# Two gated attention and feed-forward layers: split low-rank passes, one ring of three accumulator banks, and a new order of every engine's steps

## The chip, the cores and the metric

The kernel runs on one core of a Trainium2 chip. The metric is the device time of one execution in microseconds (us). A measurement of this kernel can tell a change from no change at about 0.2%.

## The reference, cut to what matters

The input `x` is 2 batches of 2048 tokens with 512 features; a context of 128 tokens per batch is given beside it. Four steps follow one another, each added to the stream with a gate:

```python
x = x + tanh(g_xattn[0]) * attention(layernorm(x), ctx)        # 8 heads, rotary, 128 keys
x = x + tanh(g_ffn[0])   * ffn_0(layernorm(x))                 # below
x = x + tanh(g_xattn[1]) * (layernorm(x) @ W1.T + mean(ctx) @ W2.T + b)
x = x + tanh(g_ffn[1])   * ffn_1(layernorm(x))                 # quantised, gelu
# ffn_0: h = ternary(w_fc)(x) + gate * (x @ v.T @ fast_b.T @ u.T);  r = relu(h);  ternary(w_proj)(r * r)
# ffn_1: h = gelu(bitlinear(x, w1, b1));  bitlinear(h, w2, b2)   # both inputs rounded to integers per token
```

The hidden width of both feed-forward parts is 2048, and the rank of the low-rank term in `ffn_0` is 16.

## The kernel before, in words

**Groups and stages.** The 4096 tokens are cut into 16 groups of 256, each of two tiles of 128 tokens. Every group goes through the same steps. On PE they are: `q` (two, queries), `s` (scores of all heads), `pv` (two, probabilities times values), `wo` (two, output projection), `low` (the low-rank rows), `up` (eight pairs of 128 hidden rows), `down` (eight pieces, four for each tile), `wx` (two, the linear step), `w1` (eight units of 512 hidden columns, four for each tile) and `w2` (two). Precision is kept by carrying most values as two f16 parts. `wx`, `w1` and `w2` are called the back stage; it trails the attention by about two groups, so that three groups are in work at a time.

**The order is written by hand.** The table `ORDER` (from line 328) gives each step of each group a place in the sequence of its engine: a row for each kind of step, in it one tuple for each group, and in the tuple a place for each step. `PREP` does so for the one-time work on the weights, which is mixed into the first groups. Each engine's `run()` walks its places in ascending order. An engine does its steps strictly in this order; a step that waits holds up all behind it. Cross-engine waits are in the helpers: `need(engine, semaphore, per, g, k)` waits until item k of group g is done, `need_dma` the same for transfers. All transfers, among them the transposes that bring a result back as a matmul input (`xT1`, `p`, `xT2`, `xT3`, `q4T`, `hT`), are issued by SP in its own order.

**Accumulator banks.** PSUM has eight banks of 512 f32 columns. Banks 0 and 1 belong to `up` and `down` (FFN0), and bank 1 takes `low` first. The attention uses 2, 3, 4 and 7 (`ATT`, `ROW_TILES`): the four score banks are 4, 7, 2, 3, and bank 7 holds nothing but the second score bank. The back stage uses 5 and 6 in turn: `wx` tile 0 and 1, `w1` units 0 to 7, `w2` tile 0 and 1. So `w1` unit u waits until DVE has emptied unit u-2 (`h_done`, L1491), and `wx` of group g waits until DVE has emptied `w2` of group g-1 (`out_done`, L1527). In the last group, where the attention is over, the back stage uses the four attention banks.

**The path through `up`.** `low` (L1744) fills bank 1; ACT copies it (L971), DVE subtracts and splits it into bf16 parts (L1420 to L1425), and `low_done` is set. Each half of an up pair is eight matmuls over `xT2` (L1764) and one low-rank matmul (L1768), so the first half of pair 0 ends with a wait for `low_done`. ACT empties a pair by two Relu (L981), and then makes two squares of it (L986, L992); pair m may start when the Relus of pair m-2 are done. POOL makes the low part of the square (L763), which `down` waits for. A score bank is emptied by a maximum on DVE (L1381), a small scale (L1385) and four Exp on ACT (L949, `s_exp`).

**Ends of a group.** `wo` is added to the input by DVE (L1407, `x1_done`), normalised, split, and transposed by DMA into `xT2`, which `low` and `up` need. `wx` is added by DVE (L1449), normalised, rounded and transposed into `q4T`, which `w1` needs (L1814). `w1`'s results go through Gelu (L1003), a maximum (L1075), rounding (L1502), a conversion (L1035) and a transpose into `hT`, which `w2` needs (L1830).

## Time and profile before

| what | value |
|---|---|
| median of 3 runs | 1218.28 us (1217.88 to 1218.72) |
| profiled execution | 1217.09 us |
| its span, first to last instruction | 1215.3 us |
| granted TensorE clock, mean | 0.977 |
| busy: PE, DVE, ACT, POOL | 91%, 79%, 65%, 49% |

The profiled execution is 1.19 us under the median, and its span is 1.8 us shorter than its own time. PE means the matmuls, PEld the weight loads that run beside them, DVE is VectorE, ACT is ScalarE, POOL is GpSimd, SP issues the transfers. An arrow in a row names what ended the idle time before an instruction. Matmul rows overlap by the drain of the array: 16 matmuls of 512 columns show 3.62 us, and the next row starts 3.45 us after their start.

### The profile page before, as it was taken

What the parts mean: (1) busy time and instruction counts of PE and PEld (TensorE: products, weight loads), DVE (VectorE), ACT (ScalarE), POOL (GpSimd) and SP (SyncE); (2) the same over time, 40 slices, a digit from 0 to 9 for tenths busy, and PEclk for the clock granted to TensorE, in tenths of its full rate; (3) what the DMA queues carried; (4) which work ended last, traced back from release to release, by engine and by line L of the source; (5) the groups of instructions that cost most, each with busy time, mean ns of one, the idle gap of its engine ahead of it and who ended that gap; (6) DMA issues with size and microseconds to landing.
All of it is one profiled execution on the core that took longest, in us unless ns stands there. A gap on an engine that the chain in (4) does not pass through costs nothing.

```text
span 1215.3 us, 22111 instructions
## 1 busy us (share of the span) xinstructions
PE 1099.9 (91%) x8254; PEld 681.4 (56%) x8542; DVE 959.9 (79%) x1993; ACT 795.2 (65%) x1557; POOL 590.3 (49%) x569
## 2 busy tenths in 40 slices
PE   5766888999999998999999989999999999999995
PEld 5544646565656555564657565654756566564642
DVE  4696689887889797888978897888869677877766
ACT  3887847666675848485756749484675929494624
POOL 2442556454546455464645465554546364563440
PEclk9878999999999999999999999999999999999997
DMA  9959472433427362435434452624345261433132
GB/s 322 361 157 280 148 195 47 95 82 81 105 48 140 57 133 55 104 80 100 88 66 105 66 128 51 126 60 102 71 79 122 48 139 34 102 70 78 23 61 65
DMA packets 281225, 129.93 MB, mean 107 GB/s; under 512 B 254992, under 2 KB 255504, under 8 KB 279440
## 3 DMA queue, kind: packets, MB, share of 16 engines
q1 hardware_dynamic: 280560, 127.57, 45.6%
q8 instruction: 66, 1.08, 0.4%
q10 hardware_dynamic: 560, 0.96, 0.3%
q14 instruction: 39, 0.32, 0.1%
HBM read 57.19 MB, written 8.39 MB: 54 GB/s over the span
## 4 chain that ended last, share of the span: by engine, by line
PE 42%; ACT 23%; DVE 22%; DMA 6%; issue 4%; POOL 3%; SPq 0%; ACTq 0%; DVEq 0%
PE ps L1780 12%; ACT e L949 5%; PE ps L1731 5%; PE ps L1814 4%; PE ps L1682 4%; PE ps L1830 4%; ACT rl L981 4%; PE ps L1764 4%; ACT hid L986 3%; ACT sq L992 2%; DVE st L1342 2%; DVE amax L1075 2%; PE ps L1797 2%; ACT p L957 1%; DMA pt<-p 1%
## 5 line engine op out<-in xcount | busy, mean ns | idle before, releaser
L1764 PE MATMUL ps<-xT,fcT 128*128 128x256 f16 x2048 | 258.7, 274 | 10.0 <-ACT rl L981 9.9
L738 POOL TENSOR_TENSOR rs<-ve,nhalf 128x1 f32<-128x1 f32 x160 | 103.8, 651 | 327.5 <-DVE ve L1347 231.0
L1780 PE MATMUL ps<-pjT,hid 128*128 128x512 fp8e4 x1024 | 232.7, 379 | 5.0 <-issue 2.7
L1764 PEld LDWEIGHTS ps<-xT,fcT 128*128 128x128 fp8e4 x2048 | 199.4, 98 | 49.0 <-ACT rl L981 13.7
L763 POOL TENSOR_TENSOR hid<-sq,hid 128x512 f16<-128x512 f32 x128 | 156.5, 1226 | 104.0 <-ACT sq L992 103.3
L1780 PEld LDWEIGHTS ps<-pjT,hid 128*128 128x128 f16 x1024 | 97.7, 98 | 98.1
L1814 PE MATMUL ps<-w1T,q4T 128*128 128x512 fp8e4 x480 | 118.5, 380 | 9.1 <-DVE h L1491 5.0
L981 ACT ACTIVATE rl<-ps,rsf 128x256 f32<-128x256 f32 x256 | 106.4, 468 | 29.7 <-PE ps L1768 29.5
L949 ACT ACTIVATE e<-ps,nmb,sig 128x128 f32<-128x128 f32 x256 | 113.1, 459 | 16.8 <-DVE nmb L1385 16.7
L1830 PE MATMUL ps<-w2T,hT 128*128 128x512 fp8e4 x480 | 108.4, 379 | 7.3 <-DMA hT<-q 7.3
L1491 DVE SCALAR_TENSOR_TENSOR h<-ps,dqs,b1bc 128x512 f32<-128x512 f32 x120 | 87.9, 743 | 25.8 <-PE ps L1814 24.8
L768 POOL TENSOR_TENSOR e<-e,einv 128x512 f32<-128x512 f32 x64 | 72.0, 1129 | 60.6 <-DVE einv L1389 60.5
L1035 ACT ACTIVATE q<-h 128x2048 f16<-128x2048 f32 x30 | 57.2, 1908 | 66.3 <-DVE h L1502 66.3
L1682 PE MATMUL ps<-pt,wq 128*128 128x256 f16 x768 | 88.6, 276 | 6.1 <-issue 4.1
L1797 PE MATMUL ps<-wx,xT 128*128 128x512 f16 x360 | 82.7, 379 | 10.0 <-DMA xT<-x16b 5.4
L1731 PE MATMUL ps<-wo,qT 128*128 128x512 f16 x384 | 85.8, 379 | 2.8 <-DVE qT L1355 2.8
L1682 PEld LDWEIGHTS ps<-pt,wq 128*128 128x128 f16 x768 | 75.4, 99 | 20.3 <-issue 10.0
L1075 DVE TENSOR_REDUCE amax<-h 128x1 f32<-128x2048 f32 x30 | 68.4, 2281 | 23.2 <-ACT h L1003 23.2
L1355 DVE TENSOR_TENSOR p<-e,p 128x512 f16<-128x512 f32 x64 | 64.2, 1014 | 25.1 <-ACT p L957 24.9
L986 ACT ACTIVATE hid<-rl 128x512 f16<-128x512 f32 x128 | 80.6, 630 | 5.0
L992 ACT ACTIVATE sq<-rl 128x512 f32<-128x512 f32 x128 | 78.5, 613 | 0.0
L1830 PEld LDWEIGHTS ps<-w2T,hT 128*128 128x128 f16 x480 | 46.1, 98 | 50.9
(234 smaller groups left out, 2032.8 us busy)
## 6 DMA issues: line engine op xcount, KB each, us to landing
xb<-in_x SPq DMA_DIRECT2D x16, 512.0 KB, 4.0
xa<-in_x SPq DMA_DIRECT2D x15, 512.0 KB, 4.0
out<-r SPq DMA_DIRECT2D x30, 256.0 KB, 2.1
rope<-in_rope SPq DMA_DIRECT2D x16, 384.0 KB, 3.4
h<-in_w1T SPq DMA_DIRECT2D x6, 1024.0 KB, 5.5
h<-in_w2T SPq DMA_DIRECT2D x6, 1024.0 KB, 5.6
h<-in_wkvT SPq DMA_DIRECT2D x2, 1024.0 KB, 12.8
hid<-in_w_fc SPq DMA_DIRECT2D x2, 1024.0 KB, 10.9
```

Source lines behind the costliest of these rows:

```text
L738: pool.tensor_tensor(rs[:, n, t:t + 1], ve[:, n, t:t + 1], nhalf[:, :], ALU.pow).then_inc(done, 1)
L763: pool.tensor_tensor(flat[:, 1, :], sq[:, m % 2, :], flat[:, 0, :], ALU.subtract).then_inc(hid_lo, 1)
L949: last = act.activation(e[:, n, a * S:(a + 1) * S], s_bank(n)[:, a * S:(a + 1) * S], ACT.Exp, bias=nmb[:, n, a:a + 1], scale=sig[:, :], ac ...
L981: act.activation(rl[:, m % 2, a * G:(a + 1) * G], ps[:, FFN0 + m % 2, a * G:(a + 1) * G], ACT.Relu, scale=rsf[:, 2 * m + a:2 * m + a + 1]) ...
L986: act.activation(hid[:, 0, 2 * m:2 * m + 2, :].rearrange("p c n -> p (c n)"), rl[:, m % 2, :], ACT.Square)\
L1682: mm = pe.matmul(q_bank(hg)[:, a * G:(a + 1) * G], wq[:, ws, k, c:c + P], xT1[:, xs, k, :], start=(n == 0 and k == 0), stop=(n == 2 and k ...
L1731: mm = pe.matmul(wo_bank(t), ao[:, xs, k, t * P:(t + 1) * P], wo[:, ws, k, :], start=(n == 0 and k == 0), stop=(n == 2 and k == KC - 1))
L1764: pe.matmul(dst, fcT[:, k, f * P:(f + 1) * P], xT2[:, xs, k, :], start=(xs == 0 and k == 0), stop=False)
L1780: mm = pe.matmul(ps[:, FFN0 + t, :], hid[:, xs, c, t * P:(t + 1) * P], pjT[:, c, :], start=(c == 0 and xs == 0), stop=(c == FC - 1 and xs ...
L1797: mm = pe.matmul(mix_bank(g, t), xT3_of(g)[:, xs, k, t * P:(t + 1) * P], wx[:, ws, k, :], start=(n == 0 and k == 0), stop=(n == 2 and k == ...
L1814: mm = pe.matmul(mix_bank(g, 2 + u), q4T_of(g)[:, k, t * P:(t + 1) * P], w1T[:, k, n * 512:(n + 1) * 512], start=(k == 0), stop=(k == KC - 1))
L1830: mm = pe.matmul(mix_bank(g, 10 + t), hT_of(g)[:, t, c, :], w2T[:, c, :], start=(c == 0), stop=(c == FC - 1))
```

## The change

Three things are done, and every order is written anew.

1. **Parted pairs.** `up` of pairs 0 and 1 does only the eight `xT2` passes of its first half. A new step `up_rest` with a place of its own waits for `low_done` and does the low-rank pass of the first half and the whole second half. Pair 0 no longer needs `low` before it in the order (it waits for `xT2` itself). Pair 1 still waits until the low-rank rows have left bank 1 (`low_r`). Pairs 2 to 7 are as before.
2. **One ring of three banks.** Banks 5, 6 and 7 form a ring in which each group has 13 slots: slot 0 is the second score bank of the group two ahead, slots 1 and 2 are `wx`, 3 to 10 are `w1`, 11 and 12 are `w2`. `w1` unit u now waits for unit u-3; unit 0 waits until ACT has done the Exp of the second score bank of the group two ahead (`s_exp` of group g+2, item 1), units 1 and 2 for `wx` of their tiles. `scores` gets a wait for the last `w1` unit of three groups before. Groups 0 and 1 keep bank 7 for their scores. In the last group the back stage has three banks (2, 3, 4) where it had four.
3. **Orders.** All places in `ORDER` and `PREP` are set anew, on all engines, with SP's transfers. PE has 630 places where it had 598. The instructions are the same in kind and number, and so are the transfers.

The diff, with the order tables cut to the rows spoken of:

```diff
@@ -168,7 +168,9 @@
         def q_bank(hg):
             return ps[:, ATT[hg], :]
 
-        def s_bank(j):
+        def s_bank(g, j):
+            if j == 1 and g >= 2:
+                return back_bank(g - 2, 0)
             return ps[:, ROW_TILES[j], :]
 
         def pv_bank(a):
@@ -177,8 +179,9 @@
         def wo_bank(t):
             return ps[:, (3, 4)[t], :]
 
-        def back_bank(n):
-            return ps[:, BACK0 + n % 2, :]
+        def back_bank(g, slot):
+
+            return ps[:, BACK0 + (13 * g + slot) % 3, :]
 
 
         hid32 = hid[:, :, :, :].rearrange("p s c n -> p (s c n)").bitcast(F32)
@@ -220,7 +223,7 @@
             return hT
 
         def mix_bank(g, n):
-            return ps[:, ATT[n % 4], :] if final(g) else back_bank(n)
+            return ps[:, 2 + n % 3, :] if final(g) else back_bank(g, 1 + n)
 
         h32 = h[:, :, :].rearrange("p t n -> p (t n)")
         hT32 = hT[:, :, :, :].rearrange("p t c n -> p (t c n)").bitcast(F32)
@@ -327,225 +330,228 @@
 
         ORDER = dict(
             PE=dict(
...
-                s=((13,), (35,), (58,), (94,), (132,), (167,), (201,), (237,), (273,), (312,), (344,), (384,),
-                   (420,), (452,), (493,), (524,)),
...
-                low=((31,), (57,), (90,), (124,), (162,), (198,), (234,), (270,), (305,), (343,), (376,), (415,),
-                     (450,), (486,), (523,), (557,)),
-                wx=((53, 56), (91, 98), (125, 135), (163, 172), (199, 204), (235, 242), (271, 276), (307, 317),
-                    (342, 352), (381, 386), (412, 422), (451, 456), (485, 495), (522, 530), (558, 560), (585, 586)),
...
-                w2=((86, 96), (123, 130), (159, 170), (195, 203), (231, 239), (267, 274), (302, 315), (339, 348),
-                    (375, 385), (408, 413), (447, 453), (483, 484), (518, 528), (555, 556), (584, 587), (596, 597))),
+                up_rest=((35, 36), (63, 64), (97, 99), (133, 134), (173, 175), (209, 212), (250, 252), (288, 291),
+                         (326, 327), (363, 364), (402, 403), (438, 441), (478, 480), (515, 516), (554, 555),
+                         (591, 593)),
+                up=((33, 34, 37, 38, 39, 40, 41, 42), (60, 62, 65, 66, 67, 68, 71, 72),
+                    (93, 98, 100, 101, 104, 105, 109, 110), (131, 132, 135, 137, 143, 144, 145, 146),
...
+                s=((13,), (31,), (61,), (102,), (141,), (179,), (215,), (249,), (287,), (328,), (366,), (405,),
+                   (444,), (481,), (525,), (556,)),
...
+                wo=((25, 27), (53, 54), (85, 86), (123, 124), (163, 165), (199, 200), (236, 237), (275, 277),
+                    (312, 313), (352, 353), (390, 391), (427, 428), (467, 468), (504, 505), (544, 545), (579, 583)),
+                low=((32,), (59,), (94,), (130,), (169,), (206,), (247,), (284,), (320,), (359,), (397,), (435,),
+                     (475,), (512,), (550,), (588,)),
+                wx=((57, 58), (96, 108), (136, 142), (168, 183), (214, 219), (246, 256), (285, 293), (324, 333),
+                    (365, 371), (396, 409), (440, 447), (472, 483), (510, 517), (552, 560), (587, 589), (617, 619)),
+                w1=((69, 70, 75, 76, 78, 79, 80, 81), (106, 107, 111, 112, 116, 119, 121, 122),
+                    (151, 152, 153, 155, 160, 161, 162, 164), (182, 186, 187, 188, 195, 196, 198, 201),
+                    (220, 221, 222, 225, 229, 230, 240, 241), (262, 263, 264, 265, 267, 268, 273, 276),
+                    (294, 297, 300, 301, 305, 310, 314, 318), (334, 335, 341, 342, 343, 344, 347, 349),
+                    (374, 375, 376, 379, 382, 383, 384, 385), (414, 415, 416, 417, 418, 419, 420, 432),
+                    (448, 450, 451, 453, 457, 458, 459, 461), (486, 487, 489, 490, 491, 492, 494, 496),
+                    (529, 531, 532, 533, 535, 536, 539, 546), (561, 564, 565, 567, 568, 570, 571, 576),
+                    (596, 597, 598, 599, 604, 605, 606, 607), (620, 621, 622, 623, 624, 625, 626, 627)),
+                w2=((90, 103), (129, 140), (167, 181), (205, 216), (243, 254), (281, 289), (319, 331), (355, 369),
+                    (394, 406), (433, 445), (469, 477), (506, 511), (549, 558), (585, 586), (616, 618), (628, 629))),
...
@@ -946,7 +952,7 @@
                     act.wait_ge(c_kap, 1)
                 need(act, s_bias, 4, g, n)
                 for a in range(4):
-                    last = act.activation(e[:, n, a * S:(a + 1) * S], s_bank(n)[:, a * S:(a + 1) * S], ACT.Exp,
+                    last = act.activation(e[:, n, a * S:(a + 1) * S], s_bank(g, n)[:, a * S:(a + 1) * S], ACT.Exp,
                                           bias=nmb[:, n, a:a + 1], scale=sig[:, :], accum_out=esum[:, n, a:a + 1])
                 last.then_inc(s_exp, 1)
 
@@ -1377,7 +1383,7 @@
 
             def soft_max(g, n):
                 need(dve, s_ps, 4, g, n)
-                scores = s_bank(n).rearrange("p (h s) -> p h s", h=4)
+                scores = s_bank(g, n).rearrange("p (h s) -> p h s", h=4)
                 dve.tensor_reduce(nmx[:, n, :], scores, axis=AX.X, op=ALU.max, negate=True).then_inc(s_max, 1)
                 if first(g) and n == 0:
                     dve.wait_ge(c_kap, 1)
@@ -1691,6 +1697,10 @@
                     pe.wait_ge(c_klo, 1)
                 if g == 1:
                     pe.wait_ge(c_mean, 1)
+                if g == 2:
+                    pe.wait_ge(c_quantp, 32)
+                else:
+                    need(pe, h_done, 4 * TILES, g - 3, 4 * TILES - 1)
                 need(pe, x1_done, TILES, g - 1, 1)
                 need(pe, q_lo, 2, g, 1)
                 b = g // PER_BATCH
@@ -1700,7 +1710,7 @@
                         for m, (half, qs, ks) in enumerate(HALVES_AND_PARTS):
                             for j in range(4):
                                 rows = slice(32 * j, 32 * j + 32)
-                                mm = pe.matmul(s_bank(j)[:, at:at + S], qT[rows, qs, hg, half, t * P:(t + 1) * P],
+                                mm = pe.matmul(s_bank(g, j)[:, at:at + S], qT[rows, qs, hg, half, t * P:(t + 1) * P],
                                                k_rows[rows, ks, 2 * hg + half, b * S:(b + 1) * S],
                                                start=(m == 0), stop=(m == 5), tile_position=(32 * j, 0))
                                 if hg == 1 and t == 1 and m == 5:
@@ -1756,17 +1766,34 @@
                     need(pe, low_r, 2, g, 0)
                 else:
                     need(pe, relu, FC, g, 2 * m - 3)
-                for a in range(2):
-                    f = 2 * m + a
-                    dst = ps[:, FFN0 + m % 2, a * G:(a + 1) * G]
-                    for xs in range(2):
-                        for k in range(KC):
-                            pe.matmul(dst, fcT[:, k, f * P:(f + 1) * P], xT2[:, xs, k, :], start=(xs == 0 and k == 0),
-                                      stop=False)
-                    if m == 0 and a == 0:
-                        need(pe, low_done, 1, g, 0)
-                    mm = pe.matmul(dst, lowA[:, f * P:(f + 1) * P], tlow[:, :], start=False, stop=True)
-                mm.then_inc(up_ps, 1)
+                if m == 0:
+                    for t in range(TILES):
+                        need_dma(pe, xT2_in[t], g)
+                up_passes(g, m, 0)
+                if m >= 2:
+                    up_rest(g, m)
+
+            def up_passes(g, m, a):
+
+                f = 2 * m + a
+                for xs in range(2):
+                    for k in range(KC):
+                        pe.matmul(ps[:, FFN0 + m % 2, a * G:(a + 1) * G], fcT[:, k, f * P:(f + 1) * P], xT2[:, xs, k, :],
+                                  start=(xs == 0 and k == 0), stop=False)
+
+            def low_pass(g, m, a):
+
+                f = 2 * m + a
+                return pe.matmul(ps[:, FFN0 + m % 2, a * G:(a + 1) * G], lowA[:, f * P:(f + 1) * P], tlow[:, :],
+                                 start=False, stop=True)
+
+            def up_rest(g, m):
+
+                if m < 2:
+                    need(pe, low_done, 1, g, 0)
+                low_pass(g, m, 0)
+                up_passes(g, m, 1)
+                low_pass(g, m, 1).then_inc(up_ps, 1)
 
             def down(g, t, piece_of_4):
                 if first(g) and piece_of_4 == 0:
@@ -1787,8 +1814,10 @@
                 if first(g) and t == 0:
                     pe.wait_ge(c_wlo, 3)
                     pe.wait_ge(c_mx, 5)
+                if first(g) and t == 1:
+                    need(pe, s_exp, 4, 1, 1)
                 if final(g):
-                    need(pe, x1_done, TILES, g, t)
+                    need(pe, x1_done, TILES, g, 1)
                 else:
                     need(pe, out_done, TILES, g - 1, t)
                 need_dma(pe, xT3_in[t], g)
@@ -1802,11 +1831,13 @@
                 u = 4 * t + n
                 if first(g) and u == 0:
                     pe.wait_ge(c_clip, 4)
-                ring = 4 if final(g) else 2
+                ring = 3
                 if u >= ring:
                     need(pe, h_done, 4 * TILES, g, u - ring)
                 elif u >= ring - 2:
                     need(pe, x3_done, TILES, g, u - ring + 2)
+                elif not final(g) and not final(g + 1):
+                    need(pe, s_exp, 4, g + 2, 1)
                 if n == 0:
                     need_dma(pe, q4T_in[t], g)
                 pe.ldweights(q4T_of(g)[:, 0, t * P:(t + 1) * P], tile_position=(0, 0))
@@ -1818,7 +1849,7 @@
             def w2_down(g, t):
                 if first(g) and t == 0:
                     pe.wait_ge(c_clip, 8)
-                need(pe, h_done, 4 * TILES, g, t + (4 if final(g) else 6))
+                need(pe, h_done, 4 * TILES, g, t + 5)
                 if final(g):
                     need_dma(pe, hT_half_in[2 * t], GROUPS)
                 else:
@@ -1834,6 +1865,8 @@
                 for p in moments("PE"):
                     for m, g in due("PE", "up", p):
                         up(g, m)
+                    for m, g in due("PE", "up_rest", p):
+                        up_rest(g, m)
                     for n, g in due("PE", "down", p):
                         down(g, n // 4, n % 4)
                     for hg, g in due("PE", "q", p):
```

## Rows read from the trace of the kernel before

**Rows 1.** The page's busy times: us, share of the span, instructions.
```profile
PE 1099.9 (91%) x8254; PEld 681.4 (56%) x8542; DVE 959.9 (79%) x1993; ACT 795.2 (65%) x1557; POOL 590.3 (49%) x569
```
**Rows 2.** Windows: length, busy of PE, PEld, DVE, ACT, POOL, PE clock, DMA share, GB/s.
```profile
0.00:100.00 100.00, 67.30 (x420) 49.89 (x420) 65.73 (x145) 70.52 (x140) 33.23 (x39) 0.86 0.85 279
100.00:200.00 100.00, 79.55 (x701) 53.19 (x710) 76.31 (x136) 69.02 (x127) 48.60 (x40) 0.93 0.60 170
200.00:1150.00 950.00, 905.22 (x6924) 556.49 (x7179) 777.66 (x1621) 628.43 (x1245) 492.52 (x475) 1.00 0.42 85
1150.00:1216.00 66.00, 47.80 (x214) 21.84 (x234) 40.19 (x93) 27.22 (x49) 15.91 (x17) 0.88 0.28 60
```
**Rows 3.** PE's waits: waiting line, what it waited for, us in total, times, longest.
```profile
PE ps L1764 <- ACT rl L981: 9.9, 10, 2.0
...
PE ps L1830 <- DMA hT<-q: 7.3, 7, 2.2
...
PE ps L1814 <- DVE h L1491: 5.0, 8, 1.4
PE ps L1797 <- DVE r L1527: 4.4, 3, 2.4
...
PE ps L1768 <- DVE tlow L1425: 3.3, 5, 0.9
...
PE ps L1780 <- ACT rl L981: 2.3, 4, 0.9
```
**Rows 4.** The tile rl: ACT's work for an up pair, ns min/median/max.
```profile
L981 ACT ACTIVATE rl<-ps,rsf x256: 452/465/518, 127.1 to 1154.8; 128x256 f32<-128x256 f32 x128
L986 ACT ACTIVATE hid<-rl x128: 629/630/632, 128.0 to 1155.3; 128x512 f16<-128x512 f32 x128
L992 ACT ACTIVATE sq<-rl x128: 612/613/617, 128.5 to 1155.8; 128x512 f32<-128x512 f32 x128
```
**Rows 5.** Timeline of PE, two up pairs in a row in the last group.
```profile
1131.53 1.04 PE L1764 MATMUL ps<-xT,fcT 128*128 128x256 f16 x8
...
1133.49 1.04 PE L1764 MATMUL ps<-xT,fcT 128*128 128x256 f16 x8
```
**Rows 6.** Timeline of PE: a `wx` that waits for its bank, a low-rank pass for `low_done`.
```profile
801.95 1.25 PE L1797 MATMUL ps<-wx,xT 128*128 128x512 f16 x5 [2.38 <-DVE r L1527]
...
931.89 0.28 PE L1768 MATMUL ps<-tlow,lowA 128*128 128x256 bf16 x1 [0.94 <-DVE tlow L1425]
```
**Rows 7.** Timeline, group 2 and group 9: the scores, and the last Exp of the second score bank.
```profile
185.65 1.52 PE L1703 MATMUL ps<-k,qT 32*128 32x128 f16 x96 [0.36 <-DVE qT L1355]
...
203.21 0.46 ACT L949 ACTIVATE e<-ps,nmb,sig 128x128 f32<-128x128 f32 x1
...
659.41 1.52 PE L1703 MATMUL ps<-k,qT 32*128 32x128 f16 x96
...
667.77 0.47 ACT L949 ACTIVATE e<-ps,nmb,sig 128x128 f32<-128x128 f32 x1
```
**Rows 8.** Timeline of the head: DVE's maximum of the `wo` weights, PE's first `wo` and `low`.
```profile
45.60 2.25 DVE L1075 TENSOR_REDUCE wmax<-pjT 128x1 f32<-128x2048 f32 x1
...
100.89 5.34 PE L1731 MATMUL ps<-wo,qT 128*128 128x512 f16 x24 [1.74 <-DVE qT L1355]
...
120.50 2.72 PE L1744 MATMUL ps<-xT,vrep 128*128 128x256 f16 x12 [5.12 <-DMA xT<-x16f]
```
**Rows 9.** Timeline of PE: the last back stage, from its first `wx` to the end.
```profile
1172.72 2.75 PE L1797 MATMUL ps<-wx,pt 128*128 128x512 f16 x12 [0.79 <-DMA pt<-x16a]
1177.51 2.75 PE L1797 MATMUL ps<-wx,pt 128*128 128x512 f16 x12 [2.04 <-DMA pt<-x16a]
1180.10 3.62 PE L1830 MATMUL ps<-w2T,hT 128*128 128x512 fp8e4 x16
1183.55 3.62 PE L1814 MATMUL ps<-w1T,qT 128*128 128x512 fp8e4 x16
1187.82 3.63 PE L1814 MATMUL ps<-w1T,qT 128*128 128x512 fp8e4 x16 [0.65 <-DMA qT<-x16a]
```

More of the change, by code:

```diff
@@ L453, in build @@
                        (514, 515)),
[L454 to L457 removed]
+                low=((56,), (86,), (114,), (145,), (176,), (207,), (242,), (271,), (301,), (331,), (362,), (393,),
+                     (425,), (457,), (488,), (517,)),
@@ new lines, in build @@
+                x2_lo=((24, 30), (52, 53), (80, 81), (113, 115), (147, 150), (182, 183), (217, 219), (252, 253),
+                       (285, 286), (319, 321), (353, 354), (387, 388), (421, 423), (454, 455), (490, 491),
+                       (520, 523)),
+                x3_lo=((47, 50), (83, 88), (111, 118), (145, 155), (180, 189), (214, 223), (247, 257), (282, 291),
+                       (316, 328), (350, 364), (384, 393), (418, 430), (451, 460), (485, 497), (519, 524),
+                       (542, 545)),
@@ new lines, in build @@
+                rot=((10, 11), (27, 29), (54, 55), (86, 87), (128, 129), (156, 159), (190, 192), (224, 225),
+                     (258, 259), (292, 293), (324, 325), (360, 361), (394, 395), (428, 429), (469, 470),
+                     (493, 494)),
+                norm=((14, 15, 16, 17), (32, 34, 41, 42), (59, 65, 69, 71), (96, 97, 99, 103), (132, 134, 139, 140),
[3 rows of a table added]
+                rs2=((22, 23), (48, 51), (76, 77), (112, 114), (146, 148), (178, 181), (212, 215), (248, 249),
+                     (280, 283), (314, 317), (348, 351), (382, 385), (416, 419), (452, 453), (488, 489),
+                     (517, 521)),
@@ L532, in build @@
                        (335, 336))))
         PREP = dict(
-            PE=dict(k=(2, 3), v=(5, 6), low=(0,), mix=(15,), tern=(4, 10, 12, 14, 17, 19, 20, 21), low_t=(18,),
-                    row_scale=(24,), mean=(30,), spread=(1, 9, 11, 16, 23)),
-            DVE=dict(ctx_sum=(11,), rot_k=(9, 10), wq_max=(4,), wq_scale=(5,), k_max=(12,), wq_lo=(7,), v_max=(17,),
-                     kv_scale=(20,), k_lo=(29,), v_lo=(34, 35), low_copy=(6,), thr=(8, 14, 21, 31, 39, 48, 49, 50),
-                     wo_max=(22,), v_top=(23,), wo_scale=(25,), wo_lo=(28,), mix_row=(43,), low_rank=(32,),
-                     v_parts=(26,), wx_max=(44,), hidden=(53,), wx_scale=(55,), wx_lo=(59,), row_scale=(57,),
-                     mean=(67,), diag=(54,), round=(68, 73, 76, 80, 86, 102, 103, 109),
-                     clip=(71, 78, 79, 94, 95, 111, 115, 116)),
@@ L542, in build @@
-            ACT=dict(wq=(3,), k_hi=(17,), v_hi=(20, 22), tanh=(0,), wo=(15,), evac=(6, 13, 16, 23, 28, 36, 37, 38),
-                     rows=(4, 7, 11, 19), whole=(5, 8, 14, 21), low=(32,), wx=(42,),
-                     sums=(27, 33, 40, 43, 44, 45, 46, 47), lift=(52, 55, 58, 74, 75, 79, 81, 85)),
-            POOL=dict(whole=(14, 19, 20, 21), rot_k=(4, 5), csb=(6,), low_zero=(13,)),
-            SP=dict(u=(1,), rows=(6,), ctx=(0,), wk=(3,), wq=(2,), wv=(7,),
-                    piece=(4, 8, 14, 20, 19, 16, 22, 24, 25, 27, 31, 34, 35, 26, 30, 38, 39, 40, 45, 46, 48, 53, 54, 58),
-                    wo=(15,), wc=(11,), wx=(5,), b1=(18,)))
+            PE=dict(k=(1, 3), v=(4, 7), low=(0,), mix=(14,), tern=(5, 8, 12, 16, 19, 20, 21, 24), low_t=(17,),
+                    row_scale=(22,), mean=(30,), spread=(2, 9, 11, 15, 26)),
@@ new lines, in build @@
+            DVE=dict(ctx_sum=(5,), rot_k=(8, 11), wq_max=(3,), wq_scale=(9,), k_max=(15,), wq_lo=(12,), v_max=(18,),
+                     kv_scale=(20,), k_lo=(29,), v_lo=(31, 32), low_copy=(6,), thr=(10, 17, 22, 38, 47, 49, 50, 51),
+                     wo_max=(7,), v_top=(21,), wo_scale=(23,), wo_lo=(26,), mix_row=(40,), low_rank=(39,),
+                     v_parts=(24,), wx_max=(43,), hidden=(54,), wx_scale=(59,), wx_lo=(67,), row_scale=(56,),
+                     mean=(70,), diag=(55,), round=(73, 76, 81, 85, 88, 90, 111, 121),
+                     clip=(75, 84, 87, 89, 96, 97, 119, 123)),
@@ new lines, in build @@
+            ACT=dict(wq=(4,), k_hi=(15,), v_hi=(18, 19), tanh=(1,), wo=(14,), evac=(6, 10, 17, 27, 35, 36, 37, 40),
+                     rows=(3, 7, 11, 20), whole=(5, 9, 13, 26), low=(30,), wx=(43,),
+                     sums=(32, 38, 41, 42, 45, 46, 49, 51), lift=(54, 57, 60, 64, 75, 76, 85, 90)),
+            POOL=dict(whole=(18, 19, 20, 21), rot_k=(5, 6), csb=(4,), low_zero=(12,)),
+            SP=dict(u=(2,), rows=(7,), ctx=(0,), wk=(3,), wq=(1,), wv=(6,),
+                    piece=(5, 10, 15, 19, 18, 17, 21, 23, 26, 30, 32, 33, 36, 29, 37, 38, 41, 42, 46, 47, 48, 50, 54, 55),
+                    wo=(4,), wc=(13,), wx=(12,), b1=(16,)))
```

217 lines of the change are left out of this document (99 added, 118 removed), and 118 rows, old and new, of tables (down, exp, h, hid).

## The prediction, made before the changed kernel was seen to run

> **What bounds the kernel now.** I read the page's busy times first, then busy times by stretch, then what PE waited for, then the timeline around those waits. PE is busy 91% of the span, DVE 79% [rows 1]. The stretches differ [rows 2]. From 200 to 1150 us PE is busy 905.2 of 950 us at a granted clock of 1.00: what is idle there is 44.8 us, and no more than that can be won by better order. The first 200 us hold 53.1 us of idle and clocks of 0.86 and 0.93; the last 66 us hold 18.2 us. So PE sets the time, and the change takes no matmul away. It can only remove waits of PE. Those waits are many and small [rows 3]: Relu on ACT (9.9 us in 10 waits, and 2.3 in front of `down`), the transposed Gelu output (7.3), a `w1` bank that DVE has not emptied (5.0), a `wx` bank still held by `w2` (4.4), `low_done` (3.3). The longest are about 2 us.
>
> How I compare two orders: PE's table says which steps lie between a step and the one that needs its result, and the spacing of rows says how long they take. Two halves of an up pair start 1.96 us apart [rows 5], 16 matmuls of 512 columns take 3.45 us, 12 take 2.59 [rows 9]. I call this the **cover** of a result. Where it is shorter than the way over the other engines, PE waits. The ways' lengths are those of this trace; under another order they may be other, which is the main doubt.
>
> **The change, part by part.**
>
> *Parted pairs.* In the first half of pair 0 PE waits for `low_done` in five groups, 3.3 us in all, 0.94 in the longest [rows 3, 6]. Now the first half of pair 1 can lie there too, 8 of an up pair's 18 matmuls, 0.87 us [rows 5]. But the new order uses this in part to pack the steps tighter: in groups 0, 3, 5 and 13 `low`, both first halves and the rest follow each other with nothing else between, so 1.7 us cover `low_done` where before mostly 2.3 to 3.5 us did. Bounds: gain 3.3, loss 2 (four groups short by 0.5). I take a gain of 1.
>
> *Relu waits.* ACT needs 2 x 0.465 + 0.630 + 0.613 = 2.17 us for a pair [rows 4], PE makes one in 1.96 [rows 5]: pairs in a row, or Exp between them on ACT, put ACT behind. For each group I set PE's cover of each pair against ACT's work in its order up to the Relu that is needed. Before, ACT comes out behind in groups 2, 4, 7, 8, 9, 11, 12 and 15 by 0.8 to 3.4 us each, 13 us with the small ones; after, from group 2 on, only by 0.7 at most, 3 us in all. Groups 0 and 1 get worse, from 9 to 12.5 us. Together 22 us short become 15. The trace paid 12.2 for the 22 [rows 3], so a third less is worth 4. Bounds: 0 and 7.
>
> *Third bank.* `w1` unit u now needs unit u-3. Where two units follow each other, cover was one unit, 0.86 us, against DVE's emptying; now it is two, 1.73 us. Of 5.0 us I take 3 (bounds 0 and 5.0). The `wx` wait of 4.4 us is three places where `w2` tile 1 stands directly before `wx` tile 1, as at 801.95 [rows 3, 6]. The ring does not remove that need, the new order does: one place with nothing between is left (`w2` tile 0 of group 2 before `wx` of group 3). Gain 3, bounds 0 and 4.4.
>
> The rows show waits of many kinds, and the two on banks are 9.4 us of them [rows 3]. The Trainium skill (Perfetto Trace Analysis, Optimization Strategy) says that one gap repeating on the engine that should be saturated can mean too few buffers in SBUF or PSUM. By that rule the third bank alone could be worth up to the steady stretch's whole idle time; by the rows it is worth at most a fifth of it, and the trace does not agree that one gap repeats.
>
> *Gelu output.* The cover of `w2` tile 1 from the last `w1` unit averages some 4 us more in the new order. Of 7.3 us [rows 3] I take 3, bounds 0 and 7.3.
>
> *The new wait.* `w1` unit 0 of group g now waits for the second score bank's Exp of group g+2. The way from the end of the scores (start plus 1.52) to the end of that Exp was 7.3 us in group 9 and 16.5 in group 2 [rows 7]; ten of the sixteen are over 8. The new order's covers are 5.4 us twice (groups 3 and 12: one up pair and one `w2` tile in group 3), 7.4, 8.0, 8.5 and ten or more in the others. In these five groups ACT's new order puts the two Exp next to each other, as in group 9, so I take 7.3: 1.9 + 1.9, with the rest near nothing 3.5. Behind the waiting unit stand `wx`, `up` and `down`, all of which wait with it. Bounds: 2 and 15 (at 9.9 us, about the middle of the sixteen). The wait added to the scores is for a `w1` unit at least 15 us back and costs nothing; cover gone, it would cost one DVE pass.
>
> *Closer inputs.* `low` of group 4 stands 7.8 us of work behind `wo` (one `down` piece, `w2`, `wx`), and in groups 5 and 14 9.5. Bounds: nothing, and the 14.3 us that lie between the end of `wo` and `low` in the head [rows 8], 6.5 us for group 4. I take a loss of 2.5, which also stands for `q` of group 2 directly behind `wo`.
>
> *Head.* DVE's maximum of `wo` (2.25 us, rows 8) leaves the stretch between the first queries and scores, its low-rank preparation goes behind the first softmax maxima, and POOL's rounding behind the normalising. The weights' load is issued earlier on SP in exchange for another of its size. The first `wo` (100.89) could start up to 7 us earlier. The rounding of `w1` and `w2` and the loads it waits for stay as long, and the head's later waits hang on them; I take 3, bounds -2 and 7. The scores of group 1 now stand ahead of the first `low`, 1.45 us, in idle that was there [rows 8].
>
> *Tail.* `w2` of group 14 now lies between the last two `wx`. The first ends at 1175.3, the second starts 3.45 us later at 1178.8 instead of 1177.51, ends at 1181.4, and unit 4 of `w1` comes 7.7 us after that, as from 1180.10 to 1187.82 [rows 9]: 1189.1, a loss of 1.3. The fourth bank, now missing there, costs nothing: two units cover a DVE pass.
>
> *SP's and POOL's queues* are renumbered by a few places, no transfer is added; nothing in both ways, and the range carries it.
>
> **Sum.** Gains 1 + 4 + 3 + 3 + 3 + 3 = 17, losses 3.5 + 2.5 + 1.3 = 7.3, net 9.7. The profiled execution took 1217.09, its span 1215.3. It becomes 1207.4; the median lies 1.2 higher: **1208.6 us**.
>
> **Rivals.** (1) *The waits only move.* PE is dense, and a wait removed lets it run into the next one, which no count by pairs of steps sees. For it: 44.8 us are spread over dozens of small waits. Against it: the gaps I name have cover to spare afterwards. Gains and losses cancel: 1217 to 1219. (2) *Slower, by the new wait.* If ACT reaches the second Exp 11 us after the scores, the places with less cover lose 3.6, 5.6, 1.0, 3.0, 2.5, 5.6 and 1.1 us, 22.4 in all, 18.9 more than taken: 1227.5. It decides from a way of about 9.5 us on; under 8 it does not. For it: the way was longer than that in most groups [rows 7]. Against it: the Exp pairs stand close in ACT's new order. (3) *Much faster*: Relu, ring, Gelu and head terms at their upper bounds, 1190 to 1197; here belongs the rule above.
>
> **How the numbers follow.** The forecast's case, 1197 to 1216, gets 0.62, rival 3 0.08, rival 1 0.13, rival 2 and kindred losses 0.17. About 0.2%, 2.4 us, is what a measurement of this kernel can tell. The range 1197 to 1222 leaves out rival 3 and about 0.1 above. Faster 0.70, same 0.13, slower 0.17.
>
> **What would show it.** PE's waits by kind: Relu under 9 us, DVE's `h` under 2.5, `wx` on DVE's output under 2, `low_done` 2 to 3, and a new line, the `w1` line waiting for ACT's Exp, at 3 to 4 us in two to five places. The first `wo` at 94 to 99 us. The window 200 to 1150 with over 910 us of PE busy at clock 1.00. The last `w1` unit 1 us later against the last `wx`. The prediction is wrong if the Exp line is over 12 us, or if the sum of PE's idle from 200 us on has not fallen.

## The result, and the profile after

The median fell from 1218.08 us (four runs beside it) to **1190.7 us** (1189.36 to 1192.99): a ratio of 0.9777, 95% interval 0.976 to 0.9794. I had forecast 1208.6 and a range from 1197. The direction was right, but the time lies outside that range: the gain was 27.4 us where I had summed 9.7.

The profiled execution took 1189.36 us, its span is 1187.5 where it was 1215.3. Busy times of the page, then windows as in [rows 2]:

```profile
PE 1095.1 (92%) x8254; PEld 681.5 (57%) x8542; DVE 951.4 (80%) x1993; ACT 794.7 (67%) x1557; POOL 592.7 (50%) x569
```
```profile
0.00:100.00 100.00, 70.68 (x442) 50.45 (x443) 67.85 (x148) 72.08 (x141) 33.16 (x40) 0.90 0.83 278
100.00:200.00 100.00, 79.55 (x714) 55.03 (x722) 79.61 (x146) 72.48 (x140) 54.29 (x45) 0.91 0.61 174
200.00:1150.00 950.00, 924.78 (x7024) 568.00 (x7291) 780.03 (x1641) 635.93 (x1245) 501.24 (x482) 1.00 0.42 87
```

From 200 to 1150 us PE is busy 924.8 us instead of 905.2, at the same clock. The instructions are the same in number, and PE needs 4.8 us less busy time for them [rows 1]. So the 27.8 us of the span are 23.0 of idle and 4.8 of busy time. Part of the latter is the clock: between 60 and 130 us 48 query matmuls take 5.40 us, the time that they take at full clock, where they took 7.07, and the granted clock of the first 100 us is 0.90 where it was 0.86. From 100 to 200 us it is 0.91 where it was 0.93, and 1.00 in the long stretch of both. That the clock is the whole of the 4.8 is not shown.

PE's waits of the kernel after, as in [rows 3]:

```profile
PE ps L1781 <- ACT rl L987: 11.3, 10, 2.2
...
PE ps L1728 <- DMA pt<-p: 8.2, 4, 6.3
...
PE ps L1861 <- DMA hT<-q: 4.7, 5, 1.4
PE ps L1713 <- DVE qT L1361: 4.6, 4, 2.9
...
PE ps L1845 <- DVE hid L1497: 3.1, 2, 1.5
...
PE ps L1845 <- DVE h L1497: 1.6, 3, 0.7
...
PE ps L1826 <- DVE r L1533: 1.2, 1, 1.2
PE ps L1754 <- DMA xT<-x16f: 1.1, 1, 1.1
...
PE ps L1845 <- ACT e L955: 0.9, 1, 0.9
...
PE ps L1787 <- DVE tlow L1431: 0.7, 2, 0.5
...
PE ps L1845 <- DMA q4T<-x16b: 0.3, 1, 0.3
PE ps L1807 <- ACT rl L987: 0.3, 1, 0.3
```

Every kind that I had named fell, Relu least. The new line, `w1` on ACT's Exp, holds 0.9 us in one wait. The row `DVE hid L1497` is also a wait for a `w1` bank: in the last group DVE writes its result into `hid`, and with three banks there `w1` waits 3.1 us that it did not wait before.

Of the signs that I had named, the first `wo` (95.11), the long stretch (924.8 us busy), `wx` on DVE's output (1.2) and the later last `w1` unit (14.6 us after the last `wx` where it was 12.9) came. DVE's `h` is at 1.6, but at 4.7 with the last group. Relu at 11.6 (forecast under 9), `low_done` at 0.7 (2 to 3) and the Exp line at 0.9 in one place (3 to 4 in two to five) did not come as said. The same view of the kernel before has kinds that I had seen and not priced:

```profile
PE ps L1703 <- DVE qT L1355: 7.8, 7, 4.1
...
PE ps L1797 <- DMA xT<-x16b: 5.4, 3, 2.7
PE ps L1744 <- DMA xT<-x16f: 5.1, 1, 5.1
...
PE ps L1797 <- DMA pt<-x16a: 2.8, 2, 2.0
...
PE ps L1814 <- DMA q4T<-x16b: 2.8, 5, 1.0
```

The two waits of `wx` (L1797) for transposes have no row after, and the other three fell from 15.7 to 6.0. Against that the head now waits 6.3 us for the first transposed probabilities (L1728); before, no such wait was longer than 0.4.

Where along the run the lead arises is read from the starts of the same steps in two timelines. `wo` of group 0 starts at 95.11 instead of 100.89 [rows 8]; `low` of group 0 is 0.7 us earlier, of group 2 8.3, of group 4 9.9, of group 8 17.4, of group 12 23.4, and `down` of the last group 27.8. So the first groups bring 8 to 10 us, groups 4 to 15 bring 18, and the last back stage brings nothing. In a second execution of the same kernel, shown further below, the first groups bring 5 to 7 and the rest the same; the last section comes back to this. The last back stage of the kernel after:

```profile
1144.21 2.75 PE L1826 MATMUL ps<-wx,pt 128*128 128x512 f16 x12
1146.80 3.62 PE L1861 MATMUL ps<-w2T,hT 128*128 128x512 fp8e4 x16
1150.25 2.75 PE L1826 MATMUL ps<-wx,pt 128*128 128x512 f16 x12
1154.46 2.76 PE L1845 MATMUL ps<-w1T,qT 128*128 128x512 fp8e4 x12 [1.45 <-DMA qT<-x16a]
1158.74 1.04 PE L1845 MATMUL ps<-w1T,qT 128*128 128x512 fp8e4 x4 [1.52 <-DVE hid L1497]
1160.57 2.76 PE L1845 MATMUL ps<-w1T,qT 128*128 128x512 fp8e4 x12 [0.79 <-DMA qT<-x16a]
```

### The profile page after: what moved, and what is told of

Its sections match the earlier page's. It is cut to its first block, busy times and chain, and to the rows that moved or that the text cites. A ratio compares the mean times of both kernels' runs of the same rounds, so it can differ in the third digit from the quotient of the medians.

```text
span 1187.5 us, 22127 instructions
## 1 busy us (share of the span) xinstructions
PE 1095.1 (92%) x8254; PEld 681.5 (57%) x8542; DVE 951.4 (80%) x1993; ACT 794.7 (67%) x1557; POOL 592.7 (50%) x569
## 4 chain that ended last, share of the span: by engine, by line
PE 50%; DVE 21%; ACT 18%; DMA 5%; issue 4%; POOL 2%; SPq 0%; DVEq 0%; ACTq 0%
PE ps L1807 14%; PE ps L1781 7%; PE ps L1845 6%; PE ps L1861 6%; PE ps L1741 5%; ACT e L955 4%; PE ps L1826 3%; ACT rl L987 3%; PE ps L1688 2%; DMA hT<-q 2%; DVE st L1348 2%; ACT sq L998 2%; PE ps L1728 2%; ACT hid L992 2%; DVE amax L1081 2%
## 5 line engine op out<-in xcount | busy, mean ns | idle before, releaser
L769 POOL TENSOR_TENSOR hid<-sq,hid 128x512 f16<-128x512 f32 x128 | 160.8, 1261 | 81.5 <-ACT sq L998 81.1
L1845 PE MATMUL ps<-w1T,q4T 128*128 128x512 fp8e4 x480 | 114.5, 379 | 2.8 <-DVE h L1497 1.6
L1497 DVE SCALAR_TENSOR_TENSOR h<-ps,dqs,b1bc 128x512 f32<-128x512 f32 x120 | 86.3, 741 | 14.6 <-PE ps L1845 12.6
L1688 PEld LDWEIGHTS ps<-pt,wq 128*128 128x128 f16 x768 | 74.4, 98 | 20.3 <-issue 11.6
## 6 DMA issues: line engine op xcount, KB each, us to landing
hid<-in_w_fc SPq DMA_DIRECT2D x2, 1024.0 KB, 12.2
```

The costliest lines, as they stand in the source:

```text
L769: pool.tensor_tensor(flat[:, 1, :], sq[:, m % 2, :], flat[:, 0, :], ALU.subtract).then_inc(hid_lo, 1)
L1688: mm = pe.matmul(q_bank(hg)[:, a * G:(a + 1) * G], wq[:, ws, k, c:c + P], xT1[:, xs, k, :], start=(n == 0 and k == 0), stop=(n == 2 and k ...
L1845: mm = pe.matmul(mix_bank(g, 2 + u), q4T_of(g)[:, k, t * P:(t + 1) * P], w1T[:, k, n * 512:(n + 1) * 512], start=(k == 0), stop=(k == KC - 1))
```

## Experiments

The question after the result: is the gain that of the orders, of the third bank or of the parted pairs, or do they only work together? All times are medians; ratios are to the kernel before, run beside each. Line numbers differ between the kernels, since their order tables differ in length: of the experiments' waits, the line in front is the `w1` matmul's.

### The three parts, one at a time

**New orders on old banks, undivided pairs.** Without a third bank the new orders do not run through: engines would wait for each other in a circle. So three steps go back behind the next three of their engine: `w1` unit 1 of group 1 on PE and its emptying on DVE, and `w1` unit 6 of group 12 on PE. (These three moves are the nine moved steps that the expectations count.) The bank functions and waits are those of before, except in the last group, which keeps three banks:

```diff
-            if j == 1 and g >= 2:
-                return back_bank(g - 2, 0)
...
-            return ps[:, BACK0 + (13 * g + slot) % 3, :]
+            return ps[:, BACK0 + (slot + 1) % 2, :]
...
-                ring = 3
+                ring = 3 if final(g) else 2
...
-                elif not final(g) and not final(g + 1):
-                    need(pe, s_exp, 4, g + 2, 1)
```

> The new orders on the old banks (back stage in a ring of two, scores in banks of their own), pairs 0 and 1 undivided at the places of their second halves; six steps of PE and three of DVE that cannot stand so with two banks are moved by one to six places, all in groups 1 to 3 and 12 to 14. Before 1218, after 1191. Theory O, the orders bring nearly all: 1193 to 1198. Theory B, the third bank is what the orders live on: 1200 to 1212, with the wait of the w1 line for DVE's h at 8 us and more instead of 1.6. Theory P, the parting counts: this kernel and the one with whole pairs on three banks both lie over 1196.

Measured: **1230.17 us**, ratio 1.0098 (1.0071 to 1.0125), slower than before and above what any theory expected of it. PE waits 28.1 us for DVE's `h`, and 6.5 for `tlow`.

**New banks under the old orders.**

> The old orders on the new banks, undivided pairs; in groups 10 to 12 the first w1 unit is put behind the scores it now waits for (seven steps of PE, four of DVE and one of ACT change places). Theory O: 1214 to 1219, the wx and h waits hardly shorter. Theory B: 1208 to 1213, since 5.0 us of waits for DVE's h can go in place. A third way, the new wait for the second Exp bites in an order not made for it: 1220 to 1230, with the w1 line waiting on Exp in several groups.

Measured: **1253.53 us**, ratio 1.0292 (1.0263 to 1.032). The third way was the right one, and larger. Its timeline shows where the `w1` unit stands and waits for the second Exp:

```profile
266.50 1.44 PE L1930 MATMUL ps<-w1T,q4T 128*128 128x512 fp8e4 x4 [4.32 <-ACT e L1037]
...
537.69 1.89 PE L1930 MATMUL ps<-w1T,q4T 128*128 128x512 fp8e4 x4 [3.10 <-ACT e L1037]
...
887.63 3.05 PE L1930 MATMUL ps<-w1T,q4T 128*128 128x512 fp8e4 x8 [4.74 <-ACT e L1037]
```

The first two belong to groups 1 and 5, where nothing was moved, the third to group 10, where it was; three more follow in groups 11 to 13, 23.4 us in all. A gap of 3.0 us in group 0 has no named releaser, but it ends 0.2 us after the last Exp of that bank, so it is the same wait. About 24 of the 36 us arise between `low` of group 11 and that of group 14, in part beside the steps that I had to move (the scores of group 12 stand some steps later for it), so the size is not that of the bank alone. The eight waits for `h` of the kernel before, 5.0 us, are all gone; the one that is there, 3.7 us at 901.27 in group 10, stands beside the steps that were moved. So the third bank does in the old orders what the rows promised, and its new wait costs several times as much.

**Parted pairs under the old orders, old banks.**

> The old orders and old banks; in each group the first halves of pairs 0 and 1 stand at the old places of the two pairs and their second halves directly behind the second one. Theory O: 1215 to 1218, 3.3 us of waits for low_done go and a little of it comes back in Relu, which now gets pair 0 later. Theory P: under 1214.

Measured: **1246.04 us**, ratio 1.0223 (1.0201 to 1.0244); both theories failed. The wait for `low_done` is gone, but the waits sum to 22.2 us more, over Relu, the scores' `qT`, `h`, `xT3` and `q4T`, and PE is busy 6.7 us longer. The starts of the steps say why: 24 of the 29 us arise in groups 3, 5, 6, 7 and 12. In these the old order has other steps (queries, scores, `w1`, `w2`, `wx`) between pairs 0 and 1, and my edit put pair 0's second half behind them. In groups 0 to 2, 4, 8, 10, 13 and 14, where the two pairs adjoin, it costs at most 0.8 us and gains nothing either. So it shows what a half pair held back costs, not what a well placed one would.

**The kernel after with undivided pairs.** The new orders and banks stay:

```diff
                 up_passes(g, m, 0)
-                if m >= 2:
-                    up_rest(g, m)
+                if m == 0:
+                    need(pe, low_done, 1, g, 0)
+                low_pass(g, m, 0)
+                up_passes(g, m, 1)
+                low_pass(g, m, 1).then_inc(up_ps, 1)
...
-                    for m, g in due("PE", "up_rest", p):
-                        up_rest(g, m)
```

> The kernel after with pairs 0 and 1 undivided, each at the place of its second half; banks and all other orders stay. Eight to sixteen matmuls (0.87 to 1.74 us) that covered the way low to low_done stand behind it: at a way of about 2.3 us nearly all of this is idle in each group. Theory O with the parting as a small term of 1: 1192 to 1196. Theory P: 1200 to 1215 (0.87 to 1.7 us in each of 16 groups).

Measured: **1194.69 us**, ratio 0.9807 (0.9782 to 0.9831). Waits for `tlow` rise from 0.7 to 6.4 us. Against the repeated kernel after (below) all waits rise by 6.5 us, and PE is busy 3.4 us less. For the comparison the kernel after was run once more:

> The kernel after unchanged, beside the next two on one chip, since the undivided-pairs kernel differs from it by less than two chips may: 1190 to 1193.

Measured: 1191.29 us, ratio 0.9776 (0.9753 to 0.98). The two intervals overlap: parting is worth 3.4 us by the medians, and by the intervals it could also be worth nothing.

### What the third bank is worth in the new orders

> The kernel after, banks as they are, only that each w1 unit waits for DVE to have emptied the unit two back instead of three back (final group unchanged); nine steps that would block each other are moved by one to six places, as in the orders-alone kernel. Theory F, the new orders live on the third bank: w1's waits for h rise from 1.6 to 25 us and more and the time to 1218 to 1230. Rival: the loss of the orders-alone kernel came from its undivided pairs and its old score bank: under 1205.

```diff
-                    need(pe, h_done, 4 * TILES, g, u - ring)
-                elif u >= ring - 2:
-                    need(pe, x3_done, TILES, g, u - ring + 2)
+                    need(pe, h_done, 4 * TILES, g, u - (3 if final(g) else 2))
+                elif u >= 1:
+                    need(pe, x3_done, TILES, g, 1)
...
-                need(pe, h_done, 4 * TILES, g, t + 5)
+                need(pe, h_done, 4 * TILES, g, t + (5 if final(g) else 6))
```

Measured: **1209.92 us**, ratio 0.9921 (0.9891 to 0.9952), between the two expectations. The edit was less than its description: unit 2 still waited only for `wx` tile 1, and unit 0 not for tile 0. Two more kernels closed that gap.

> The orders-alone kernel with its pairs 0 and 1 parted again: new orders and parting on the old banks. It lacks, against the wait-of-two kernel (1209.9), the score bank in the ring and with it the new wait. If the undivided pairs cost little with any banks, as they did with three (4 us): 1224 to 1228. If the 20 us between the orders-alone kernel and the wait-of-two kernel are what undivided pairs cost when DVE holds the banks too: 1206 to 1212.

Measured: **1228.13 us**, ratio 1.008 (1.0054 to 1.0105). So on two banks the parting hardly counts (1230.17 without it, other runs of before beside it), and of the two expectations the first is the right one, its upper end just passed.

> New banks and new waits, but every wait inside the back stage as with a ring of two. The wait-of-two kernel left the third unit and the first one free of theirs (the third waited for the second wx tile alone); here unit 0 also waits for wx tile 0, unit 1 for wx tile 1 and unit 2 for unit 0's h. The orders of all engines are those of the new orders on the old banks (1228). If what the third bank brings is the freedom of the w1 units alone: 1225 to 1230 and 28 us of waits for h. If the 18 us between 1209.9 and 1228 come from the score bank that stands for itself on the old banks: 1208 to 1213 and 16 us of waits for h.

Measured: **1226.04 us**, ratio 1.0058 (1.0038 to 1.0077). It has three banks, the scores in the ring and the new wait, and still loses 35 us against after, by the waits and the three moved steps. The orders of this kernel, of the old-banks kernel and of the kernel with waits of two in part are the same on every engine, so the 16 us from 1209.92 to 1226.04 are those of waits alone. The rows, in the order of waits of two in part, of two throughout, and of the old banks:

```profile
PE ps L1930 <- DVE h L1582: 16.2, 11, 3.8
```
```profile
PE ps L1930 <- DVE h L1582: 27.4, 15, 4.2
```
```profile
PE ps L1920 <- DVE h L1580: 28.2, 16, 4.2
```

No run has the three moved steps with the waits of three, so their own price is not measured. It is bounded by where the 35 us arise: of the lag behind the repeated kernel after, 3.0 us arise between `low` of group 2 and of group 3 and 8.8 between those of groups 13 and 14, the stretches in which the moved steps lie; the other 23 arise where no step was moved. So it is the freedom of the `w1` units from DVE that the new orders live on, for two thirds of the loss at least. Where the score bank lies makes no difference that the runs can tell (ratios 1.0058 and 1.008, intervals overlapping); it is only the place that the third bank came from. The accounts close: against the repeated kernel after, the old-banks kernel waits 25.3 us more (114.9 to 89.6) and is busy 11.4 us more (1107.5 to 1096.1), and its span is 36.8 us longer.

### How near the new wait is to costing something

```diff
-                    need(pe, s_exp, 4, g + 2, 1)
+                    need(pe, s_exp, 4, g + 2, 2)
```

> The kernel after, with the new wait made longer: the first w1 unit waits for the third Exp of group g+2, one bank further than it must. If the second Exp arrives with cover to spare in nearly all groups (0.9 us of wait in the trace after): 1190 to 1195. If the new wait is near its limit in many groups, as it was in the old orders on new banks (23.4 us in six waits): 1197 to 1210.

Measured: **1229.54 us**, ratio 1.007 (1.0041 to 1.0099). One Exp later, a wait of 0.9 us becomes 25.9 in eight waits, the longest 6.85. A further gap of 6.9 us at this line, in group 0, has no named releaser; it ends 0.2 us after the Exp of the third bank. Both expectations were too low. The largest belongs to group 3, one of the two places where I had reckoned the least cover. It is shown in windows around it (columns as in [rows 2]) and in the timeline:

```profile
406.00:413.00 7.00, 0.24 (x2) 0.00 (x0) 1.41 (x3) 6.29 (x19) 3.66 (x3) 0.67 0.31 75
413.00:416.00 3.00, 2.91 (x7) 1.08 (x9) 0.75 (x1) 1.75 (x8) 0.00 (x0) 0.50 0.00 0
416.00:419.00 3.00, 3.00 (x9) 1.11 (x8) 0.00 (x0) 0.00 (x0) 0.00 (x0) 0.56 0.00 0
419.00:422.00 3.00, 3.00 (x28) 2.55 (x26) 2.28 (x7) 0.56 (x2) 0.46 (x1) 1.00 0.01 3
```
```profile
413.09 1.89 PE L1930 MATMUL ps<-w1T,q4T 128*128 128x512 fp8e4 x4 [6.85 <-ACT e L1040]
414.77 4.66 PE L1911 MATMUL ps<-wx,xT 128*128 128x512 f16 x12
419.27 1.04 PE L1866 MATMUL ps<-xT,fcT 128*128 128x256 f16 x8
```

ACT is busy 6.29 of the 7 us: it was doing its Relu and softmax work, in the order fixed for it, on the way to that Exp. And PE pays more than the wait, see the last section.

### Where the gain arises

Old orders up to a point, new ones from there, on all engines, with the new banks and parted pairs throughout. The cut is the set of steps that are done when PE ends the `low` named.

> The kernel after, but every engine keeps the old order for all that was done by the time PE ends the first low pass, and the new order from there on. After reached that point only 0.7 us earlier than before, though its first wo stood 5.8 us earlier. Theory: the head as such brings 1 to 2, so 1191 to 1194. Rival: work that the new head leaves for later or brings forward is paid in groups 0 and 1, where after gains 7 us more: 1197 to 1200.

Measured: **1197.63 us**, ratio 0.9819 (0.9789 to 0.985). The rival was right: by the ratios the head is worth 5 us, by the medians 6 to 7, though the intervals of this kernel and of after just overlap. From `down` of group 1 to the end this kernel runs 6.8 to 7.9 us behind the first profile of after, and 3.8 to 5.1 behind the second.

> As the kernel before it, with the change of orders at the low pass of group 4. After was 9.9 us ahead there. If gains stay where they arise: 1200 to 1203, and the traces' later part runs as in after. If the new wait costs something in the old orders of groups 0 to 3, as it did in six places of the old orders: up to 1212. If the lead of the early groups is given back later anyway: 1191 to 1195.

Measured: **1211.8 us**, ratio 0.9931 (0.9911 to 0.9952): the second expectation. The old orders of groups 0 to 3 run into two of the new waits (3.7 us in group 1, and 3.1 in group 0 in a gap that ends 0.2 us after the last Exp of the bank; the 0.9 of group 12 is there as in after), and `low` of group 4 starts 10.5 us later than before. From the first piece of `down` of group 4 to the end it gains 19.7 us on before, and after gains 20.0 there. **In these two kernels gains stay where they arise**: the later groups neither give back nor take up what the earlier ones did.

### The last group

```diff
-            return ps[:, 2 + n % 3, :] if final(g) else back_bank(g, 1 + n)
+            return ps[:, (2, 3, 4, 5)[n % 4], :] if final(g) else back_bank(g, 1 + n)
...
-                ring = 3
+                ring = 4 if final(g) else 3
+                if final(g) and u == 1:
+                    need(pe, h_done, 4 * TILES, g - 1, 7)
...
-                need(pe, h_done, 4 * TILES, g, t + 5)
+                need(pe, h_done, 4 * TILES, g, t + (4 if final(g) else 5))
```

> The kernel after with four banks in the ring of the final group, as before (banks 2 to 5, the unit that takes bank 5 waits for the last h of group 14). In the trace after the w1 line waits 3.1 us for h in the final group, where it did not wait before. If DVE's passes set the pace there, a fourth bank only moves the wait and the last h comes when it came: within 0.5 of after. If the bank is what it waits for: 1.5 to 3 less than after.

Measured: 1192.56 us, ratio 0.9779 (0.9755 to 0.9803), against 1191.29 and 0.9776 beside it. The wait for `w1` banks in that group, 3.1 us in the first profile of after and 1.5 in the second, goes to nothing. The wait for the second tile's transposed inputs grows from 0.8 to 2.5 us, so most of it only moves. From the last group's first `wx` to the end this kernel takes 42.4 us, and the repeated kernel after 42.7.

## Why the prediction was right in direction and wrong in size

The five kinds of waits that I tied to a part of the change, with the new wait, were forecast to bring 10.5 us (1 + 4 + 3 + 3 + 3 - 3.5), and PE's waits fell by 11.5 in them. That this agrees is in part luck: Relu was 3.4 too high, the new wait 2.6 too dear, the parting 1.6 too low. The miss is in the rest. For the head, closer inputs and the tail I had -0.8, and nothing for all other kinds of waits and for PE's busy time. There the waits fell by 11.4 us, 6.6 of it before 200 us and 4.6 in the long stretch, and PE's busy time by 4.8. The step that failed is that I costed only what a part of the change names, and took the other kinds of waits and PE's busy time as fixed.

By stretches, from the waits and busy times:

| stretch | forecast, us | measured, us |
|---|---|---|
| up to 200 us | 1 (head 3, less 2 of Relu) | about 8: waits 52.9 to 49.7, and the 4.8 of busy time |
| 200 to 1150 | 10 | 19.4 (waits 43.8 to 24.4) |
| last back stage | -1.3 | 0 |

*Parted pairs* (forecast 1): the waits for `low_done` fell from 3.3 to 0.7, and the removal costs 3.4 by the medians. A little low.

*Relu* (4): 12.2 became 11.6. After 200 us it fell from 8.4 to 3.7, in the first groups it rose from 3.7 to 7.9. I had seen both movements; the second was nearly as large as the first, where I had taken it for 2.

*Third bank and `wx`* (3 and 3): 5.0 became 1.6 and 4.4 became 1.2, so 3.4 and 3.2; against the 3.4 stand the 3.1 us of the last group, which the fourth bank had kept away. *Gelu output* (3): 7.3 became 4.7. These terms were right as counts. But they priced the third bank by the waits for banks in the kernel before, 5 us, and taking it from the kernel after costs 35 to 37, of which 12 arise where steps were moved. An order planned on two banks has already kept its `w1` units apart and shows little waiting for them. Groups 0 to 14 have 90 units with a unit two back. In the kernel before none of them starts within 1.8 us of that unit and 31 start within 4.5; in the kernel after it is 21 and 48. The Trainium skill (Perfetto Trace Analysis, Optimization Strategy) says that a gap repeating on the engine that should be saturated can be a lack of buffers. I weighed it against the rows, and the rows won: no such gap repeats in the kernel before. The runs side with neither. The bank alone makes the kernel slower, and without it the new orders lose the whole gain and 10 us more.

*The new wait* (-3.5) was a term mis-sized: 0.9 (1.7 in the repeated kernel, with 0.8 in group 0). Its two dear places have the cover that I reckoned, 5.4 us in group 3 and 5.5 in group 12, but the ways are 4.6 and 6.2 us in the trace after, not 7.3, so the waits are nothing and 0.9, not 1.9 each. (Of the sixteen ways of the kernel before eleven are over 8 us, not ten; it changes nothing.) I had taken 7.3 from an old group for a path whose order on ACT was new. The mechanism of rival 2 is real, and the runs show its size: 23.4 us in an order not made for it, 25.9 one Exp later. That it did not decide here is the work of the new orders.

*Closer inputs* (-2.5): `low` waits 2.3 us for its inputs over the whole run and waited 7.9; `q` on `x1` rises from 2.0 to 3.9, and `up` waits 0.8 for `xT2`. In the long stretch the three nearly cancel (-1.6, +1.3 and +0.8). No loss where I took 2.5.

*What had no term* is the largest part of the miss. I costed the kinds of waits that I could tie to a part of the change, 32.2 us of 110.7. The rest, above all waits of `wx` and `w1` for transposes and of the scores for DVE, fell too, by 4.6 us in the long stretch. And I had written that the change can only remove waits of PE, which put its busy time at no change: it fell by 4.8 us (3.7 in the repeated kernel). When every order is new, every kind of wait is up for change.

*Head* (3): the runs give 5 to 7. The first `wo` came 5.8 us earlier in one execution and 2.9 in the other, within the 7 that I had allowed. I had looked no further than that. At `low` of group 0 the kernel with the old head is still 1 to 4 us ahead of the two profiles of after, and at `low` of group 1 it is 4 to 7 us behind. So the head's gain comes between the two; which of the moved steps bring it stays open.

*Tail* (-1.3): `w2` of group 14 between the two `wx` costs 1.2 us there, as reckoned: the lead is 28.5 us at the first `wx` and 27.3 at the second. Before that it had risen by 0.6, since the first `wx` no longer waits for its transposes [rows 9], and by the end it is 27.7. That the fourth bank is worth nothing was right.

The chances: I gave the right case, rival 3, 0.08. For it stood that its upper bounds were all within the trace. But the gain did not come by its terms: Relu stayed far from its bound, and what it lacked were the rest of the waits and the busy time.

## What to carry to other kernels

An order fitted to its resources hides what those resources cost: in this kernel the waits for a bank, 5 us, told what the third bank removes under the old order, and not what it is worth to a new one. Where an order and a resource change together, price them together, and look at the parts by taking each one away from the kernel after; adding them one at a time to the kernel before gave +2.9%, +2.2% and +1.0% (banks, parting, orders), and their sum is no guide to the -2.2% of all three. When all orders are new, the sum has to run over all kinds of waits, those that no part of the change names among them.

## What the runs showed of the hardware that was not expected

**A long wait of PE costs more than its length.** The wait of 6.85 us in the long stretch begins with PE at a granted clock of 1.00; within it, from 410 to 413 us, the clock is 0.50, the lower of the two levels (1.2 GHz). In the two windows after it it is 0.50 and 0.56, and 12 `wx` matmuls take 4.66 us where they take 2.75 at full clock (above). A wait of 4.16 us for `h` in the kernel with waits of two throughout is followed by 5 us at 0.50, in which eight `up` matmuls take 1.92 us where they take 1.04. The same shows in the sums: with the waits of 119.5, 114.9 and 134.3 us in the third-Exp, old-banks and banks-alone kernels, PE's busy time for the same matmuls is 1105.3, 1107.5 and 1112.5 us, and 1096.1 in the repeated kernel after. So a quarter to a third of what these three lost against the repeated kernel after is busy time. The Trainium skill (TensorE: Matmul & The Clock Gate, Part 1) has a clock that is low by default and is released by activity; these rows agree. My rival 2 had priced its waits at their length alone, and so had I every other term.

**The head varies between executions by 3 us, and the difference stays.** The same kernel started its first `wo` at 95.11 us in one execution and 2.9 us later in the other:

```profile
98.02 2.75 PE L1826 MATMUL ps<-wo,qT 128*128 128x512 f16 x12
```

From there to the end the two run 2.4 to 3.4 us apart, with spans of 1187.5 and 1190.3. Over all profiles the first `wo` starts at 99.0 to 100.9 us in the five kernels with the old head and at 95.1 to 98.3 in the nine profiles with the new one. So of the lead of 5.8 us that the two profiles compared first show there, about half lies within what two executions of one kernel differ by. A single profile of such a kernel places steps in the head to no better than 3 us.
